# First layer of the experts: four fp32r products over stacked high and low parts, or two fp32 products of 64 rows each

## The reference

```python
x = iter_norm_whiten(x)                      # 64x64 whitening over all tokens, 5 iterations
t = to_tokens(x)
t = t + attn(ln(t))                          # window of 33 keys, softmax, layernorm
u = ln(t)                                    # tokens of the experts
logits = u @ router_w.T ; top 2 of 8, renormalised -> combine[N, 8]
out = u
for e in range(8):
    h = gelu(u @ w1[e] + b1[e])              # 64 -> 64
    y = h @ w2[e] + b2[e]                    # 64 -> 64
    out = out + combine[:, e:e + 1] * y
t = t + out
```

## Time and profile before

| | us |
|---|---|
| median of 3 runs | 1121.23 |
| lowest, highest | 1112.76, 1134.49 |
| profiled execution | 1112.64 |
| its span | 1110.9 |
| TensorE matmuls busy | 1048.4 (94%) |
| VectorE busy | 904.3 (81%) |
| ScalarE busy | 565.4 (51%) |

### The profile page before, as it was taken

The page is one execution under the profiler, slowest core; times in us unless marked ns, Lnnn a source line. Parts: engine busy times, 40 slices in busy tenths (PEclk is TensorE's granted clock), DMA queues, the critical chain, the costliest instruction groups (busy, mean ns, idle before and its releaser), DMA issues.

```text
span 1110.9 us, 26094 instructions
## 1 busy us (share of the span) xinstructions
PE 1048.4 (94%) x9158; PEld 692.8 (62%) x9158; DVE 904.3 (81%) x2575; ACT 565.4 (51%) x917; POOL 148.3 (13%) x179
## 2 busy tenths in 40 slices
PE   7947999999999999998799999999999999999998
PEld 7935777777777777776455555555555555555553
DVE  6944888887888887887788888888888888888785
ACT  0014655655566555653455555555555555555553
POOL 7021232232223222231000000000000000000000
PEclk9959999998999999995799999999999999999999
DMA  9604555554555555543122222222222222222221
GB/s 290 238 9 105 142 131 147 136 133 113 143 138 136 142 135 137 136 120 90 42 67 70 71 66 67 71 70 66 74 66 67 68 73 66 70 71 66 67 71 44
DMA packets 244750, 111.51 MB, mean 100 GB/s; under 512 B 199392, under 2 KB 242656, under 8 KB 243888
## 3 DMA queue, kind: packets, MB, share of 16 engines
q1 hardware_dynamic: 235456, 96.91, 35.1%
q10 hardware_dynamic: 8064, 12.85, 3.4%
q0 software_dynamic: 1136, 0.56, 0.2%
HBM read 71.60 MB, written 38.67 MB: 99 GB/s over the span
## 4 chain that ended last, share of the span: by engine, by line
PE 82%; ACT 9%; DVE 4%; issue 3%; DMA 2%; SPq 0%; POOL 0%; DVEq 0%; ACTq 0%; POOLq 0%
PE p L1138 17%; PE p L1113 16%; PE p L1123 10%; PE p L1087 7%; PE p L971 7%; ACT prob L569 5%; PE p L1060 4%; PE p L964 4%; PE p L981 4%; ACT xt_s L521 3%; PE p L1082 3%; DMA resid<-in_x_dram 2%; PE p L1134 2%; PE p L979 2%; PE p L1008 2%
## 5 line engine op out<-in xcount | busy, mean ns | idle before, releaser
L586 ACT ACTIVATE arena<-p,b_s 128x896 f32<-128x896 f32 x224 | 225.5, 1007 | 231.0 <-PE p L1113 229.6
L890 DVE TENSOR_TENSOR arena<-arena,p 128x896 f32<-128x896 f32 x224 | 242.5, 1083 | 76.4 <-PE p L1123 74.8
L1138 PE MATMUL p<-arena,w_s 128*64 128x448 f32 x896 | 215.2, 559 | 0.3 <-DVE arena L890 0.3
L1113 PE MATMUL p<-thl,w_hi 128*128 128x448 f32 x448 | 165.2, 450 | 0.4 <-DVE thl L862 0.4
L1113 PE MATMUL p<-thl,w_lo 128*128 128x448 f32 x448 | 127.3, 365 | 0.0
L1123 PE MATMUL p<-arena,selector 128*128 128x448 bf16 x448 | 123.9, 358 | 1.8 <-DVE arena L890 1.4
L1123 PEld LDWEIGHTS p<-arena,selector 128*128 128x128 bf16 x448 | 25.4, 97 | 159.0 <-issue 116.9
L1113 PEld LDWEIGHTS p<-thl,w_hi 128*128 128x128 f32 x448 | 85.6, 192 | 21.2 <-issue 0.6
L479 POOL TENSOR_TENSOR yb<-yb,bet 128x448 f32<-128x448 f32 x56 | 59.2, 1058 | 253.5 <-DVE xn_s L828 253.5
L569 ACT ACTIVATE prob<-p 96x896 f32<-96x896 f32 x56 | 51.1, 912 | 78.2 <-PE p L1087 78.2
L1113 PEld LDWEIGHTS p<-thl,w_lo 128*128 128x128 f32 x448 | 84.9, 189 | 7.6
(11 more groups left out here) (177 smaller groups left out, 1640.6 us busy)
## 6 DMA issues: line engine op xcount, KB each, us to landing
tn_spill<-tnt_s ACTq DMA_DIRECT2D x56, 224.0 KB, 2.7
arena<-tn_spill SPq DMA_DIRECT2D x56, 224.0 KB, 3.4
t_s<-tn_spill SPq DMA_DIRECT2D x56, 224.0 KB, 2.5
arena<-in_x_dram SPq DMA_DIRECT2D x112, 96.0 KB, 2.6
xn_rows<-xn_s SPq DMA_DIRECT2D x56, 192.0 KB, 2.1
out_dram<-arena SPq DMA_DIRECT2D x112, 96.0 KB, 1.8
resid<-in_x_dram SPq DMA_DIRECT2D x6, 1568.0 KB, 14.2
v_a<-xn_rows SPq DMA_DIRECT2D x56, 168.0 KB, 3.3
```

Source lines behind the costliest of these rows:

```text
L586: a.activation(hid[:, j % 2, :].rearrange("p (h n) -> p h n", h=H), (p34 if j % 2 == 0 else p56)[:, :, 0:CH], ACT.Gelu, bias=b1_s[:, j:j + ...
L890: v.tensor_tensor(gated[:, j % 2, :].rearrange("p (h n) -> p h n", h=H), hid[:, j % 2, :].rearrange("p (h n) -> p h n", h=H), p01[:, :, 0: ...
L1113: last = t.matmul(bank[:, h, 0:CH], w[:, 128 * j:128 * (j + 1)], thl[:, c, h, :], start=(k == 0), stop=(k == 1))
L1138: last = t.matmul(p2[64 * h:64 * h + 64, 0:CH], w2_s[:, j, :], gated[:, j % 2, h * CH:(h + 1) * CH], start=False, stop=(j == 3))
```

## The change

The first layer takes the tokens as they lie in the spill: half h in partitions 64h to 64h + 63, in fp32. The weights are one fp32 tile `w1_s`, standing twice below each other. For half h one product with K = 64 reads partitions 64h to 64h + 63 of both. The high and low parts of tokens and weights go, with ScalarE's and VectorE's steps that make them; one load of a chunk's tokens serves the first layer and `together`. SyncE starts it when `together` of the chunk two before is done. TensorE's loop over chunks is written out.

```diff
-        w1_hi = sb("w1_hi", [128, E * C], f32r)
-        w1_lo = sb("w1_lo", [128, E * C], f32r)
+        w1_s = sb("w1_s", [128, E * C])
...
-        tn_in = carve(at3, [2, H * CH], rows=64)
+        tn_in = carve(at3, [2, CH])
...
-            def rows(g, c):
-                wait(sp, s_y3s, g - 1)
-                sp.dma_start(tn_rows[:, c, :], spill[g]).then_inc(s_tr[c], 16)
-
             def step3(g, c, has):
                 if has(0):
-                    wait(sp, s_hi, g - 1)
-                    wait(sp, s_lo, g - 1)
-                    sp.dma_start(tn_in[:, c, :].rearrange("p (h n) -> p h n", h=H),
-                                 spill[g].rearrange("(h p) n -> p h n", h=H)).then_inc(s_ti[c], 16)
-                    if not isinstance(g, int):
-                        rows(g, c)
+                    wait(sp, s_y3s, g - 1)
+                    sp.dma_start(tn_in[:, c, :], spill[g]).then_inc(s_ti[c], 16)
...
-            act.wait_ge(s_wc, 1)
-            a.activation(w1_hi[:, :], w1_f, ACT.Copy).then_inc(s_ca, 1)
...
-            def high(g, c, n):
-
-                wait(act, s_ti[c], 16 * n)
-                wait(act, s_h, 4 * (g - 1))
-                a.activation(thl[0:64, c], tn_in[:, c].rearrange("p (h n) -> p h n", h=H), ACT.Copy).then_inc(s_hi, 1)
...
-            v.scalar_tensor_tensor(w1_f, p01[:, 0, 0:E * C], -0.5 / C, w1_f, ALU.mult, ALU.add).then_inc(s_wc, 1)
+            v.scalar_tensor_tensor(w1_s[:, :], p01[:, 0, 0:E * C], -0.5 / C, w1_f, ALU.mult, ALU.add).then_inc(s_wc, 1)
...
-            dve.wait_ge(s_ca, 1)
-            v.tensor_tensor(w1_lo[:, :], w1_f, w1_hi[:, :].bitcast(f32), ALU.subtract)
...
-            def low(g, c):
-                wait(dve, s_hi, g + 1)
-                v.tensor_tensor(thl[64:128, c], tn_in[:, c].rearrange("p (h n) -> p h n", h=H),
-                                thl[0:64, c].bitcast(f32), ALU.subtract).then_inc(s_lo, 1)
...
-                v.tensor_tensor(y3, p2[:, 0:CH], tn_rows[:, cq, :], ALU.add).then_inc(s_y3s, 1)
+                v.tensor_tensor(y3, p2[:, 0:CH], tn_in[:, cq, :], ALU.add).then_inc(s_y3s, 1)
...
                 if j == 0:
-                    wait(pe, s_lo, g + 1)
+                    pe.wait_ge(s_ti[c], 16 * (g // 2 + 1))
                 wait(pe, s_g, u - 1)
-                for k, w in enumerate((w1_hi, w1_lo)):
-                    for h in range(H):
-                        last = t.matmul(bank[:, h, 0:CH], w[:, 128 * j:128 * (j + 1)], thl[:, c, h, :],
-                                        start=(k == 0), stop=(k == 1))
+                for h in range(H):
+                    r = slice(64 * h, 64 * h + 64)
+                    last = t.matmul(bank[:, h, 0:CH], w1_s[r, 128 * j:128 * (j + 1)], tn_in[r, c, :], start=True, stop=True)
                 last.then_inc(s_h, 1)
...
-            step3(1, 1, lambda d: d <= 1)
-            with pe.Fori(1, G // 2 - 1) as i:
-                step3(i * 2, 0, lambda d: True)
-                step3(i * 2 + 1, 1, lambda d: True)
-            step3(G - 2, 0, lambda d: True)
-            step3(G - 1, 1, lambda d: True, more=False)
-            step3(G, 0, lambda d: d > 0, more=False)
+            for g in range(1, G + 1):
+                step3(g, g % 2, lambda d, g=g: d <= g < G + d, more=g + 1 < G)
```

More of the change, by code:

```diff
@@ L176, in hybrid_kernel @@
         cparts = carve(at3, [2, NB * CP], bf16)
[L180 to L183, removed]
+        yb = sb("yb", [128, CPI, NB, C + 1])
         xt_s = sb("xt_s", [128, CH])
@@ L197, in hybrid_kernel @@
         top = sb("top", [128, 5, NB * CPI])
-        tn_rows = t_s[:, 0:2, :, :].rearrange("p k b c -> p k (b c)")
         p01 = pb("p01", [128, 2, 512])
@@ L229, in hybrid_kernel @@
         s_ti = [sem(f"tn_in{i}") for i in range(2)]
-        s_tr = [sem(f"tn_rows_in{i}") for i in range(2)]
-        s_hi, s_lo, s_cs, s_cpt = sem("tn_hi"), sem("tn_lo"), sem("comb_steps"), sem("comb_parts")
+        s_cs, s_cpt = sem("comb_steps"), sem("comb_parts")
         s_ct, s_cts, s_ctd = sem("comb_t"), sem("comb_t_copied"), sem("comb_t_doubled")
@@ L395, in _ @@
             sp.wait_ge(s_t2, G)
-            for c in range(2):
-                rows(c, c)
             with sp.Fori(1, G // 2) as i:
@@ L505, in _ @@
             a.preload_act_table_set("natural_log_exp_and_others")
-            act.wait_ge(s_wc, 1)
-            a.activation(w1_hi[:, :], w1_f, ACT.Copy).then_inc(s_ca, 1)
             act.wait_ge(s_cd, 10)
             a.activation(small1[0:64, 3:4], small1[0:64, 0:1], ACT.Ln).then_inc(s_ca, 1)
-            act.wait_ge(s_ca, 2)
+            act.wait_ge(s_ca, 1)
             a.activation(small1[0:64, 4:5], small1[0:64, 3:4], ACT.Exp, scale=-0.5).then_inc(s_ca, 1)
@@ L607, in share, with step3 @@
                     a.activation(top[:, 3, :], top[:, 2, :], ACT.Tanh, scale=0.5).then_inc(s_gexp, 1)
-            def step3(g, c, has, i, first=0):
+            def step3(g, has, first=0):
+                c = g % 2
                 if has(0):
@@ L614, in step3 @@
                 if has(0):
-                    if not (isinstance(g, int) and g + 1 >= G):
-                        high(g + 1, 1 - c, i + 1 + c)
                     gelu(g, c, 2)
@@ L619, in step3 @@
                     share(G + 7 + g, 1)
-                    if not (isinstance(g, int) and g + 1 >= G):
+                    if g + 1 < G:
                         double(g + 1, 1 - c)
@@ L626, in _ @@
                 if c == 3:
-                    act.wait_ge(s_t2, G)
-                    high(0, 0, 1)
                     a.preload_act_table_set("gelu_and_others")
@@ L636, in _ @@
                     gelu(0, 0, 0)
-            step3(0, 0, lambda d: d <= 0, 0, first=1)
+            step3(0, lambda d: d <= 0, first=1)
             for g in range(1, G + 1):
-                step3(g, g % 2, lambda d, g=g: d <= g < G + d, g // 2)
+                step3(g, lambda d, g=g: d <= g < G + d)
         @blk.vector
@@ L704, in _ @@
                 link(v.scalar_tensor_tensor(psig[0:64, 0, :], p7[0:64, 0:C], -0.5, p15[0:64], ALU.mult, ALU.add))
-            dve.wait_ge(s_ca, 3)
+            dve.wait_ge(s_ca, 2)
             link(v.tensor_tensor(small1[0:64, 5:6], small1[0:64, 0:1], small1[0:64, 4:5], ALU.mult))
@@ L903, in step3 @@
                                 parts_step(g + 1, 1 - c, 4)
-                                low(g + 1, 1 - c)
                             if has(1):
@@ L934, in stored @@
             def stored(eng, q, cq):
[L936 to L939, removed]
+                wait(eng, s_out[cq], 16 * MOVES * (q // 2))
             for c in range(7):
@@ L949, in _ @@
                         parts_step(0, 0, k)
-                    low(0, 0)
             dve.wait_ge(s_t2, G)
```

## The result

The changed kernel takes 1163.0 us (median of 4 runs, 1151.0 to 1174.75) beside 1117.49 us of the kernel before (4 runs, 1112.76 to 1134.49). The ratio is 1.0386, 95% interval 1.0265 to 1.0508: slower. It leaves out the slowest run of each kernel (1174.75 and 1134.49 us), which lies over 1.5% above that kernel's fastest and counts as a run in a slow state. The forecast was 1156 us, within 1140 to 1180; against the then known median of 1121.23 us that is a ratio of 1.031, and the sum itself, 1152.1 / 1112.64, gives 1.0355.

The account below looks back on a forecast made before the run. TensorE alone was taken to bound the expert stage. +41 us for its chunks, less 1.1 and 0.5, gave +39.5: 1152 us from the profiled 1112.64, 1161 from the median; 1156 was given, range 1140 to 1180.

Parts of the forecast that it names:

- Term 1: Expert stage: dropping ScalarE's high part and VectorE's low part gains 0, since TensorE waits for neither.
- Term 2: First layer: fp32 row halves stream side by side, 0.75 against 0.81 us, a gain of 0.06 us a quarter.
- Rival A: First layer: row halves share too much; +101 us if slowed by 1.6, +168 us if one after the other; chance 0.10.
- Term 3: Array-shape switch, 0.094 us, and bare weights, 0.107 us, before each quarter's first layer; also a switch and bare weights before back transposes.
- B: First layer: the shape switch is free and weights are prefetched, leaving only the shorter stream; 1099 us; chance 0.04.
- C: First layer: the switch gap stays but weights are prefetched through it; +14 us, 1125 us; chance 0.09.
- Term 4: Sum of an expert-stage chunk on TensorE: 10.02 becomes 10.75 us, times 56 chunks, +41 us.
- Term 5: Tokens' load, moved behind the residual sum, lands before the next first layer with 2.3 us to spare: 0.
- Rival D: The tokens' load comes late for the first layer; +56 us at 1 us late in each chunk; chance 0.01.
- Term 6: TensorE's chunk loop written out costs 0, bounds -1 and +5 us.
- Term 7: Prologue without w1's high and low parts on VectorE: -1.1 us; where the experts begin: -0.5 us.

Follow-up runs that it names:

- the fifth run: Changed kernel with the spread of the combine weights also made by two 64-row products side by side: 1072.14 us, ratio 0.9596 to the kernel before.

## Why the prediction was right

- Bound: TensorE alone in stage three. The run without the parts shows it, and so does gelu's longer wait after the change.
- Term 1, relief of ScalarE and VectorE: 0 said, 0 measured. The condition beside it, that the cover goes only when TensorE gets below 8.6 us a chunk, was too simple: with half of the columns TensorE waits for VectorE at 9.26 us, though VectorE is busy for only 7.5 us of a chunk (318.70 of 400 us). When a step comes in VectorE's order counts too, not only the sum.
- Term 2, streams: 0.75 us a quarter from the second layer's rate. The pairs follow at 0.48 less 0.11 = 0.37 us, and half of the columns take 0.37 us less. Rival A (0.10) is out.
- Term 3, switch and bare weights: 0.094 + 0.107 us said; 0.10 and 0.11 read, 0.21 as the fixed part with half of the columns. For the back transposes 0.149 said, 0.15 measured. Rivals B and C are out: the gap is there and nothing is loaded in it. What the rows of other pairs of shapes showed (96x96 to 64x96, 128x64 to 128x128) carried over to this one unchanged.
- The rule of the Trainium skill that I weighed there (TensorE: Matmul & The Clock Gate, Part 3: weight loads overlap running matmuls only in other row groups) would have added 24 us. The second pair reloads the row groups of the first, and comes 0.37 us of stream after it: the trace disagrees here as well. The same section also lets a load go ahead into a background weight buffer, and the 0.37 us fit that.
- Term 4, a chunk: 10.75 us said, 10.75 measured; stage three +41 said for 56 chunks, +39.7 measured over its 55 intervals.
- Term 5, the load: 0 said; it lands 3.2 us ahead of need. Rival D is out.
- Term 6, the written-out code: 0 said, 0 measured.
- Term 7: prologue -1.1 said, 2.08 - 0.99 = 1.09 measured. The entry to stage three: from the last part of the combine weights (536.03) to the end of the eight first-layer instructions (540.62) were 4.6 us, now 557.77 to 561.52, 3.75: 0.84 us for 0.5. The eight were themselves shorter, 2.94 for 3.33 us. In this profile the gain does not last: from there to the next combine transpose it is 10.49 us for 8.61, of which the longer chunk explains only part; the mean granted clock there is 0.67 for 0.80.
- The base: between 1152 (a quick execution) and 1161 (the median) I gave 1156; the median came out at 1163.0. The 1156 was a choice between two bases and not worked out, so that it came within 7 us of the median is in part luck; the sum is tested by the +39.7 of stage three and the 38.4 and 41.8 us between runs of like clock. The four runs of the changed kernel had mean clocks of 0.941 to 0.962, the slowest the lowest and the fastest the highest. That clock varies from run to run with either kernel; what sets it these runs do not show.

## What to carry to other kernels

On TensorE, count the changes of array shape, not only the streams: here a product made of two row halves side by side streamed twice as fast as on the full array (0.75 for 1.50 us), and paid 0.20 us at 2.4 GHz where the product before it had another shape, half of it for the gap and half for weights that were not loaded ahead. So change neighbours together: here one edit of the first layer lost 4%, and with the spread in the same shape the pair of edits won 4%. Time taken off engines that wait for TensorE showed up as their waiting. Whether it is of use at 9.19 us a chunk, where VectorE would without the relief be busy for 8.6 us, no run here separates.

## What was not expected of the hardware

Four fp32r instructions of 448 columns take 0.81 us, 0.20 each, and four fp32 ones 1.50 us, 0.375 each, which is less than twice that. One pass of 448 columns at 2.4 GHz is 0.187 us, so by this estimate the fp32 stream, two passes an instruction, has no step between instructions, and the fp32r stream has one of 0.015 us. Bare bf16 weights for 64 rows cost some 0.01 us after a switch (0.29 us of the spread in the fifth run, less 0.09 of gap and 0.19 of stream), fp32 ones of as many columns 0.11 us.
